# Graph attention with layer norm: both heads' quarters side by side in the moves, loads and stores of two tiles

## The chip, the cores and the metric

The kernel runs on one core of one Trainium2 chip. The metric is device microseconds of one launch; the kernel before took 1819.06 us, the median of three runs.

## What is computed

The reference, cut to what matters. There are 8 graphs of 1024 nodes with 384 features, 6 heads of 64 features, and a dense mask of 1024 x 1024 per graph.

```python
q = heads(x @ Wq + bq); k = heads(x @ Wk + bk); v = heads(x @ Wv + bv)
scores = einsum('bhqd,bhkd->bhqk', q, k) / sqrt(64)
probs = softmax(scores + where(adj, 0, -9e15), axis=-1)
ctx = einsum('bhqk,bhkd->bhqd', probs, v)
out = layernorm(x + merge(ctx) @ Wf + bf)
```

All data is float32. Projections and scores are built from three products of rounded high parts and low rests.

## The kernel before

The work of a batch (one graph) is cut into 24 slots. A slot is 128 queries of one pair of heads: slot `s` has group of queries `s // 6` (256 queries), pair `s % 6 // 2` and query tile `s % 2`. Two slots that share a pair and a group of queries make one mix (`GROUPS`, 12 in a batch). The batches are three bodies of program text: the first batch, a loop over six, and the last batch.

In a slot PE makes the scores of both heads (L494, `score_ps`, 128 x 1024 per head). DVE adds the mask and takes the row's minimum (`mask_scores`, L680), ACT takes the exponential and the row sum (`exponential`, L602), and DVE transposes every square of 32 x 32 in place (`turn_squares`, L688). All three work in `prob`, a ring of three slots with two rows of 1024 keys per partition, one for each head.

A whole transposition also needs the squares to change places between partitions. That is done by DMA: `move_square(queue, s, a, c)` (L290 to L295) takes 32 partitions and a quarter of the keys (256) of both heads from `prob`, and puts them into 32 other partitions of `prob_t`. There are 16 such moves in a slot, one for each pair of source quarter `a` and target quarter `c`. SP issues the twelve with `a != c` (`move`, L331), ACT the four with `a == c` (L612). Each move raises `landed[ring]` by 16. PE then mixes: for 8 tiles of keys and 2 heads it multiplies `prob_t` with `v_all` (`mix`, L499 to L512), each time with a moving operand of 8 runs of 32 columns.

The order of everything else is written out by hand. `STEADY` says which projections, mixes (`m`), spreads of the inverse row sums (`i`) and output projections (`p`) stand in which slot on PE; ACT, DVE and GpSimd follow the same table. SP's queue has, behind the moves of a slot, what four tables and a rule give it, one tile (128 rows) at a time: `load_adjacency` at slots 0 and 1 of every six, `X_LOADS`, `STORES`, `RES_LOADS`. Every one of them waits on a semaphore first, and everything queued behind on SP waits with it:

- `move` waits for DVE's squares (`squared`), and in even slots for the mix of two groups before (`mixed`), since `prob_t` has two halves;
- `store` (L358) waits for GpSimd's scaling of the tile (`normalised`, L286), which `NORMALISE` puts at slots 3, 10, 13 and 18;
- `load_residual` (L351) waits for the store from the same place, `load_x` (L341) for the transpositions on PE that read `x_in`, `load_adjacency` (L325) for GpSimd's mask from the same tile.

DVE's mask of a slot waits for the moves of the slot three before (`landed`), since it writes the same place of the ring.

Of the kernel before, what the change touches and what calls it, by code (L numbers as in the profile page):

```python
# [104 lines left out]
def graph_attention(nc, x, adj, wq, bq, wk, bk, wv, bv, wf, bf, out):  # L105
# [15 lines left out]
    with ExitStack() as ctx:  # L121
# [19 lines left out]
        prob = sb("prob", [P, 2 * RING, S], F32)  # L141
        prob_t = sb("prob_t", [P, 2, 2, 2, 4, GQ], F32)
# [25 lines left out]
        bv_wide = prob[:, 2 * RING - 1, 0:FT * P].rearrange("p (t n) -> p t n", t=FT)  # L168
# [13 lines left out]
        x_loaded = [sem(f"x_loaded{i}") for i in range(4)]  # L182
        res_loaded = [sem(f"res_loaded{g}") for g in range(4)]
        adj_loaded = [sem(f"adj_loaded{i}") for i in range(2)]
# [97 lines left out]

        def scale_rows(engine, group):
# [18 lines left out]
        def _(sp):  # L302
# [4 lines left out]
            for i in range(4):  # L307
                sp.dma_start(x_in[:, i, :], x_tiles[0, :, i, :]).then_inc(x_loaded[i], 16)
            for g in (2, 3):
                sp.dma_start(res[:, 2 * g:2 * g + 2, :], x_tiles[0, :, 2 * g:2 * g + 2, :]).then_inc(res_loaded[g], 32)  # L310
# [4 lines left out]
            for qt in range(2):  # L315
                sp.dma_start(adj_in[:, qt, :], adj_rows[qt * P:(qt + 1) * P, :]).then_inc(adj_loaded[qt], 16)
# [3 lines left out]
            for g in range(2):  # L320
                sp.dma_start(res[:, 2 * g:2 * g + 2, :], x_tiles[0, :, 2 * g:2 * g + 2, :]).then_inc(res_loaded[g], 32)
# [19 lines left out]
            def load_x(b, half, i):  # L341
                last_x = ("x", FT - 1, 1 - half, 1)
                if half == 0 and b.mode == "first":
                    sp.wait_ge(job_done, 3)
                else:
                    sp.wait_ge(job_done, done_through(b, last_x, 1 - half))
                    sp.sem_inc(sp_waited, 1)
                row = S + (4 * half + i) * P
                sp.dma_start(x_in[:, i, :], x_rows[bass.ds(at(b, S, row), P), :]).then_inc(x_loaded[i], 16)  # L349

            def load_residual(b, group, tile, ahead):  # L351
                sp.wait_ge(stored[group], at(b, 32, 32 * ahead))
                sp.sem_inc(sp_waited, 1)
                n = 2 * group + tile
                sp.dma_start(res[:, n, :], x_rows[bass.ds(at(b, S, ahead * S + n * P), P), :]  # L355
                             ).then_inc(res_loaded[group], 16)

            def store(b, group, tile):  # L358
                sp.wait_ge(normalised, at(b, TT, 2 * group + tile + 5))
                sp.sem_inc(sp_waited, 1)  # L360
                n = 2 * group + tile
                sp.dma_start(out_rows[bass.ds(at(b, S, n * P), P), :], res[:, n % TT, :]).then_inc(stored[group % 4], 16)  # L362

            def body(b):
                for s in range(SLOTS):
                    move(b, s)
                    if s % 6 < 2 and (s // 6 < 3 or b.mode != "last"):
                        load_adjacency(b, s // 6, s % 6)
                    if s in X_LOADS and b.mode != "last":
                        load_x(b, *X_LOADS[s])  # L370
                    if s in STORES and (STORES[s][0] >= 0 or b.mode != "first"):
                        store(b, *STORES[s])
                    if s in RES_LOADS:
                        group, tile = RES_LOADS[s]
                        if group >= 2 and b.mode != "first":
                            load_residual(b, group, tile, 0)
                        if group < 2 and b.mode != "last":
                            load_residual(b, group, tile, 1)
# [6 lines left out]
            for group in (2, 3):  # L385
                for tile in range(2):
                    store(last, group, tile)
            for g in range(4):
                sp.wait_ge(stored[g], 32 * BATCH)
# [3 lines left out]
        def _(pe):  # L393
# [66 lines left out]
            def run(b, job):  # L460
                bank_free(b, job)
                kind, n, piece, ahead = job
                if kind == "x":
                    if n == 0:
                        for i in range(4):
                            pe.wait_ge(x_loaded[i], at(b, 32, 16 * piece + 32) if piece == 0 else at(b, 32, 48))
# [32 lines left out]
            def mix(b, group):  # L499
# [25 lines left out]
            for n, job in enumerate(START_JOBS):  # L525
                if n == 0:
                    for i in range(4):
                        pe.wait_ge(x_loaded[i], 16)
                if n == 3:
                    for g in (2, 3):  # L530
                        pe.wait_ge(res_loaded[g], 32)
# [22 lines left out]
        def _(act):  # L554
# [42 lines left out]
            def exponential(b, t):  # L597
# [4 lines left out]
                nc.scalar.activation(prob[:, ring, :], prob[:, ring, :], ACT.Exp, scale=-1.0,  # L602
# [49 lines left out]
        def _(dve):  # L652
# [18 lines left out]
            def mask_scores(b, t):  # L671
# [8 lines left out]
                nc.vector.tensor_tensor_reduce(prob[:, ring, :], score_ps[:, head, :], mask[:, s % 2, :],  # L680
# [3 lines left out]
            def turn_squares(b, t):  # L684
                ring = 2 * (t // 2 % RING) + t % 2
# [86 lines left out]
        def _(pool):  # L772
# [8 lines left out]
            def next_mask(b, group, qt):  # L781
                pool.wait_ge(adj_loaded[qt], at(b, 64, 16 * (group + 1)))
# [4 lines left out]
            def residual(b, g):  # L787
                pool.wait_ge(res_loaded[g], at(b, 32, 32))
# [77 lines left out]
            nc.gpsimd.memset(ones[:], 1.0).then_inc(ones_done, 1)  # L866
            for qt in range(2):
                pool.wait_ge(adj_loaded[qt], 16)
# [28 lines left out]
```

## Time and profile before

| | us |
|---|---|
| median of three runs | 1819.06 |
| the three runs | 1817.99, 1819.06, 1821.70 |
| the profiled execution | 1816.15 |
| its span, first to last instruction | 1814.0 |

The profile is of one execution. Its span leaves out 2.15 us around the program. "Busy" counts the instructions of an engine, not its semaphore, register and DMA-issuing work; an engine's queue is written with a q (SPq, ACTq), and the chain and the timelines do show the time that it takes to issue a DMA. Line numbers are those of the kernel before.

### The profile page before, as it was taken

Reading aid. Unit: us, or ns where it says so; the run is one execution under the profiler, and the core shown is the slowest. Engines: PE = TensorE matmul, PEld = TensorE weight load, DVE = VectorE, ACT = ScalarE, POOL = GpSimd, SP = SyncE. Lnnn points to the kernel's source line nnn. Section 1 sums busy time; section 2 is a strip of 40 time slices with the busy share of each in tenths; the row PEclk is TensorE's granted clock in tenths of the full one; section 3 lists DMA queues with packets and bytes.
Section 4 is the critical chain, followed back from the end, with each engine's and each line's share of the span. In section 5 each row is a group of like instructions: output and inputs, shape, how many; then the busy total and the mean of one; then the engine's idle time right before and its main releaser. Section 6 shows DMA issues by size and latency. Waiting matters only on the chain.

```text
span 1814.0 us, 29642 instructions
## 1 busy us (share of the span) xinstructions
PE 1345.2 (74%) x8406; PEld 951.3 (52%) x8406; DVE 1059.9 (58%) x1617; ACT 722.3 (40%) x1404; POOL 655.0 (36%) x958
## 2 busy tenths in 40 slices
PE   7767796767967689676886677866888667887773
PEld 5545574545745457444574455644556445565542
DVE  5565665655656546565555655556556565566752
ACT  5443542434434434344443434434344344443330
POOL 2233541434314433154331543325433154342332
PEclk9897998878988889888898878978789788898977
DMA  5555555555555555555555555555555555555552
GB/s 154 138 136 146 144 136 141 135 151 143 128 140 140 148 139 126 142 138 149 143 128 143 139 143 141 128 140 142 146 139 132 141 146 143 144 130 149 144 137 78
DMA packets 285113, 251.62 MB, mean 139 GB/s; under 512 B 54400, under 2 KB 284928, under 8 KB 284928
## 3 DMA queue, kind: packets, MB, share of 16 engines
q1 hardware_dynamic: 223488, 199.07, 43.1%
q10 hardware_dynamic: 61440, 50.38, 11.4%
q8 instruction: 80, 1.31, 0.3%
q14 instruction: 105, 0.86, 0.2%
HBM read 35.33 MB, written 12.58 MB: 26 GB/s over the span
## 4 chain that ended last, share of the span: by engine, by line
SPq 76%; issue 10%; PE 5%; DVE 2%; ACTq 2%; ACT 2%; DMA 1%; POOL 1%; POOLq 0%; DVEq 0%
SPq L293 70%; PE context_ps L510 2%; ACTq L293 2%; DVE prob L688 2%; SPq L362 1%; SPq L329 1%; SPq L355 1%; PE score_ps L494 1%; DMA prob_t<-prob 1%; ACT prob L602 1%; SPq L349 1%; PE job_ps L399 0%; DMA x_in<-in_x_dram 0%; PE job_ps L401 0%; PE job_ps L400 0%
## 5 line engine op out<-in xcount | busy, mean ns | idle before, releaser
L510 PE MATMUL context_ps<-prob_t,v_all 128*64 128x256 f32 x3072 | 490.8, 489 | 306.5 <-DMA prob_t<-prob 306.4
L602 ACT ACTIVATE prob<-prob,row_min 128x1024 f32<-128x1024 f32 x384 | 439.6, 1146 | 530.5 <-DVE row_min L680 462.8
L680 DVE CUSTOM_DVE_ANT_0 prob<-score_ps,mask 128x1024 f32<-128x1024 f32 x384 | 454.2, 1220 | 214.0 <-PE score_ps L494 162.8
L510 PEld LDWEIGHTS context_ps<-prob_t,v_all 128*64 128x64 f32 x3072 | 301.3, 180 | 496.2 <-issue 386.7
L688 DVE STREAM_TRANSPOSE prob<-prob 128x1024 f32<-128x1024 f32 x384 | 457.9, 1231 | 151.4 <-ACT prob L602 151.4
L809 POOL TENSOR_TENSOR diag<-ident,inv_sum 128x512 f32<-128x512 f32 x96 | 99.9, 1040 | 488.4 <-DVE inv_sum L693 487.0
L610 ACT ACTIVATE context_hi<-context 128x256 fp32r<-128x256 f32 x96 | 40.1, 418 | 510.2 <-DVE context L698 385.5
L698 DVE TENSOR_TENSOR context<-context_ps,context 128x256 f32<-128x256 f32 x96 | 40.1, 418 | 317.6 <-PE context_ps L510 317.6
L803 POOL TENSOR_TENSOR q_lo<-raw,q_hi 128x256 fp32r<-128x256 f32 x95 | 69.3, 730 | 360.0 <-ACT raw L594 360.0
L399 PE MATMUL job_ps<-xt_hi,weight_hi 128*128 128x256 f32 (+1 forms) x423 | 149.4, 353 | 24.6 <-ACT raw L592 24.0
L494 PE MATMUL score_ps<-k_hi,q_hi 64*128 64x512 f32 x768 | 145.3, 457 | 20.6 <-DVE row_min L680 16.5
L401 PE MATMUL job_ps<-xt_hi,weight_lo 128*128 128x256 f32 (+1 forms) x423 | 137.1, 324 | 0.0
L400 PE MATMUL job_ps<-xt_lo,weight_hi 128*128 128x256 f32 (+1 forms) x423 | 137.0, 324 | 0.0
L494 PE MATMUL score_ps<-k_lo,q_hi 64*128 64x512 f32 x768 | 123.5, 399 | 0.0
L494 PE MATMUL score_ps<-k_hi,q_lo 64*128 64x512 f32 x768 | 122.5, 396 | 0.0
L399 PEld LDWEIGHTS job_ps<-xt_hi,weight_hi 128*128 128x128 f32 x423 | 80.9, 191 | 71.6 <-issue 36.7
L286 POOL TENSOR_SCALAR res<-res,mean_var,inv_dev 128x384 f32<-128x384 f32 x64 | 105.0, 1647 | 6.9 <-POOL inv_dev L834 6.9
L430 PE MATMUL job_ps<-diag,ones 128*64 128x256 f32 x384 | 67.8, 434 | 53.4 <-POOL diag L809 53.4
L494 PEld LDWEIGHTS score_ps<-k_hi,q_hi 64*128 64x128 f32 x768 | 59.5, 192 | 83.4 <-issue 60.8
L815 POOL TENSOR_TENSOR context_lo<-context,context_hi 128x256 fp32r<-128x256 f32 x96 | 70.5, 735 | 84.8 <-ACT context_hi L610 84.8
L803 POOL TENSOR_TENSOR k_lo<-raw,k_hi 128x512 fp32r<-128x512 f32 x46 | 58.3, 1288 | 116.1 <-ACT raw L594 116.1
L401 PEld LDWEIGHTS job_ps<-xt_hi,weight_lo 128*128 128x128 f32 x423 | 81.3, 192 | 6.7
(72 smaller groups left out, 1709.2 us busy)
## 6 DMA issues: line engine op xcount, KB each, us to landing
prob_t<-prob SPq DMA_DIRECT2D x2304, 64.0 KB, 2.0
prob_t<-prob ACTq DMA_DIRECT2D x768, 64.0 KB, 2.1
out_dram<-res SPq DMA_DIRECT2D x64, 192.0 KB, 2.1
x_in<-in_x_dram SPq DMA_DIRECT2D x60, 192.0 KB, 2.6
res<-in_x_dram SPq DMA_DIRECT2D x56, 192.0 KB
adj_in<-in_adj_dram SPq DMA_DIRECT2D x64, 128.0 KB, 2.1
res<-in_x_dram SPq DMA_DIRECT2D x4, 384.0 KB
prob_t<-in_L_gnn_Wk_dram SPq DMA_DIRECT2D x1, 576.0 KB, 3.9
```

Source lines behind the costliest of these rows:

```text
L286: engine.tensor_scalar(res[:, n, :], res[:, n, :], mean_var[:, group % 2, tile, 0:1], inv_dev[:, group % 2, tile:tile + 1], ALU.subtract, ...
L293: queue.dma_start(prob_t[32 * c:32 * c + 32, group % 2, :, qt, a, :], prob[32 * a:32 * a + 32, 2 * ring:2 * ring + 2, GQ * c:GQ * c + GQ]) ...
L399: pe.matmul(dst, left_hi, right_hi, start=(t == 0), stop=False)
L400: pe.matmul(dst, left_hi, right_lo, start=False, stop=False)
L401: last = pe.matmul(dst, left_lo, right_hi, start=False, stop=(t == FT - 1))
L494: last[head] = pe.matmul(score_ps[:, head, keys], q_part[rows, pair, q], k_part[rows, pair, keys], start=(n == 0), stop=(n == 2))
L510: last = pe.matmul(context_ps[64 * head:64 * head + 64, 0:GQ], v_all[:, kt, col:col + HS], keys, start=(kt == 0), stop=(kt == TT - 1))
L602: nc.scalar.activation(prob[:, ring, :], prob[:, ring, :], ACT.Exp, scale=-1.0, bias=row_min[:, ring:ring + 1], accum_out=row_sum[:, s // ...
L680: nc.vector.tensor_tensor_reduce(prob[:, ring, :], score_ps[:, head, :], mask[:, s % 2, :], 1.0, HUGE, ALU.add, ALU.min, row_min[:, ring:r ...
L688: nc.vector.transpose(prob[:, ring, :], prob[:, ring, :]).then_inc(squared, 1)
L803: nc.gpsimd.tensor_tensor(lo, copy[:, 0:width], hi, ALU.subtract).then_inc(lo_done, 1)
L809: nc.gpsimd.tensor_tensor(diag[:], ident[:].unsqueeze(1).to_broadcast([P, 4, P]), inv_sum[:, group % 2, :].unsqueeze(2).to_broadcast([P, 4 ...
```

## The change

`prob` is laid out anew: ring, quarter of keys, head, 256 keys. What a move takes from one partition, a quarter of both heads, is then one run of 512 numbers (2 KB) instead of two of 256. `prob_t` is laid out alike, so that it is one run there too. The number of moves, their bytes, their queues and their order stay. DVE's mask and transposition and ACT's exponential address a head as four pieces of 256 instead of one of 1024, and PE's moving operand steps over 512 numbers between its runs of 32 instead of 256.

Besides, loads of x, of residuals and of adjacency, and the stores, take two tiles (256 rows) in one issue. The tables say at which slots; most pairs go where their second tile went. The semaphores count accordingly.

```diff
-STORES = {5: (-2, 0), 6: (-2, 1), 12: (-1, 0), 13: (-1, 1), 15: (0, 0), 16: (0, 1), 19: (1, 0), 20: (1, 1)}
-RES_LOADS = {8: (2, 0), 9: (2, 1), 14: (3, 0), 15: (3, 1), 18: (0, 0), 19: (0, 1), 22: (1, 0), 23: (1, 1)}
-X_LOADS = {1: (0, 0), 2: (0, 1), 3: (0, 2), 4: (0, 3), 11: (1, 0), 12: (1, 1), 13: (1, 2), 14: (1, 3)}
+STORES = {5: -2, 12: -1, 16: 0, 20: 1}
+RES_LOADS = {8: 2, 15: 3, 19: 0, 23: 1}
+X_LOADS = {2: (0, 0), 4: (0, 1), 11: (1, 0), 14: (1, 1)}
...
-        prob = sb("prob", [P, 2 * RING, S], F32)
-        prob_t = sb("prob_t", [P, 2, 2, 2, 4, GQ], F32)
+        prob = sb("prob", [P, RING, 4, 2, GQ], F32)
+        prob_t = sb("prob_t", [P, 2, 2, 4, 2, GQ], F32)
...
+        def probabilities(t):
+            return prob[:, t // 2 % RING, :, t % 2, :]
...
-            queue.dma_start(prob_t[32 * c:32 * c + 32, group % 2, :, qt, a, :],
-                            prob[32 * a:32 * a + 32, 2 * ring:2 * ring + 2, GQ * c:GQ * c + GQ]
+            queue.dma_start(prob_t[32 * c:32 * c + 32, group % 2, qt, a].rearrange("p h n -> p (h n)"),
+                            prob[32 * a:32 * a + 32, ring, c].rearrange("p h n -> p (h n)")
                             ).then_inc(landed[ring], 16)
...
-            def load_adjacency(b, group, qt):
-                sp.wait_ge(mask_done, at(b, TT, 2 * group + qt + 1))
+            def load_adjacency(b, group):
+                sp.wait_ge(mask_done, at(b, TT, 2 * group + 2))
                 sp.sem_inc(sp_waited, 1)
-                row = (group + 1) * GQ + qt * P
-                sp.dma_start(adj_in[:, qt, :], adj_rows[bass.ds(at(b, S, row), P), :]).then_inc(adj_loaded[qt], 16)
+                sp.dma_start(adj_in[:], adj_rows[bass.ds(at(b, S, (group + 1) * GQ), GQ), :].rearrange(
+                    "(q p) k -> p q k", p=P)).then_inc(adj_loaded, 16)
...
-            def store(b, group, tile):
-                sp.wait_ge(normalised, at(b, TT, 2 * group + tile + 5))
+            def store(b, group):
+                sp.wait_ge(normalised, at(b, TT, 2 * group + 6))
                 sp.sem_inc(sp_waited, 1)
-                n = 2 * group + tile
-                sp.dma_start(out_rows[bass.ds(at(b, S, n * P), P), :], res[:, n % TT, :]).then_inc(stored[group % 4], 16)
+                n = 2 * group
+                sp.dma_start(out_rows[bass.ds(at(b, S, n * P), GQ), :].rearrange("(t p) h -> p t h", p=P),
+                             res[:, n % TT:n % TT + 2, :]).then_inc(stored[group % 4], 16)
...
-                    if s % 6 < 2 and (s // 6 < 3 or b.mode != "last"):
-                        load_adjacency(b, s // 6, s % 6)
+                    if s % 6 == 1 and (s // 6 < 3 or b.mode != "last"):
+                        load_adjacency(b, s // 6)
...
-                        keys = prob_t[:, group % 2, head, :, :, 32 * kt:32 * kt + 32].rearrange(
+                        keys = prob_t[:, group % 2, :, :, head, 32 * kt:32 * kt + 32].rearrange(
...
-                nc.scalar.activation(prob[:, ring, :], prob[:, ring, :], ACT.Exp, scale=-1.0,
+                nc.scalar.activation(probabilities(t), probabilities(t), ACT.Exp, scale=-1.0,
...
-                nc.vector.tensor_tensor_reduce(prob[:, ring, :], score_ps[:, head, :], mask[:, s % 2, :],
+                nc.vector.tensor_tensor_reduce(probabilities(t), in_quarters(score_ps[:, head, :]),
+                                               in_quarters(mask[:, s % 2, :]),
...
-                nc.vector.transpose(prob[:, ring, :], prob[:, ring, :]).then_inc(squared, 1)
+                nc.vector.transpose(probabilities(t), probabilities(t)).then_inc(squared, 1)
```

`load_x` and `load_residual` are changed as `store` is. How SP's queue reads is shown at one place, slots 12 and 13 of the loop body, where loads of adjacency and of x and a store stand behind the moves. "ISA" and "REGISTER_ALU" rows are work on the registers that carry addresses and semaphore values. Before:

```order
L293 DMA prob_t<-prob 32x2x256 x12
L326 REGISTER_ALU
L329 ISA
L329 DMA adj_in<-in_adj_dram 128x1024
L349 ISA
L349 DMA x_in<-in_x_dram 128x384
L362 ISA
L362 DMA out_dram<-res 128x384
L332 REGISTER_ALU
L293 DMA prob_t<-prob 32x2x256 x12
```

And now (L301 is the move, L371 the store, L336 the adjacency):

```order
L301 DMA prob_t<-prob 32x512 x12
L371 ISA
L371 DMA out_dram<-res 128x2x384
L340 REGISTER_ALU
L301 DMA prob_t<-prob 32x512 x12
L334 REGISTER_ALU
L336 ISA
L336 DMA adj_in<-in_adj_dram 128x2x1024
L340 REGISTER_ALU
L343 REGISTER_ALU
L301 DMA prob_t<-prob 32x512 x12
```

After slot 12 stood three issues of one tile and stands one of two; the adjacency has gone to slot 13, where three more stood before. On DVE no instruction changes its place; the two that work in `prob` change their shape. Before:

```order
L680 ISA prob,row_min<-score_ps,mask 128x1024
L680 ISA row_min 128x1
L680 ISA prob,row_min<-score_ps,mask 128x1024
L680 ISA row_min 128x1
L688 STREAM_TRANSPOSE prob<-prob 128x1024 x2
```

And now, in the first slot of the first batch like the rows above:

```order
L689 ISA prob,row_min<-score_ps,mask 128x4x256
L689 ISA row_min 128x1
L689 ISA prob,row_min<-score_ps,mask 128x4x256
L689 ISA row_min 128x1
L697 STREAM_TRANSPOSE prob<-prob 128x4x256 x2
```

The same five instructions, a head in four pieces.

## Rows read from the trace of the kernel before

**Rows 1.** The page's head and part 1: engine, busy us (share) xinstructions.

```profile
span 1814.0 us, 29642 instructions
...
PE 1345.2 (74%) x8406; PEld 951.3 (52%) x8406; DVE 1059.9 (58%) x1617; ACT 722.3 (40%) x1404; POOL 655.0 (36%) x958
```

**Rows 2.** The page, part 4: the chain that ended last, by engine, by line.

```profile
SPq 76%; issue 10%; PE 5%; DVE 2%; ACTq 2%; ACT 2%; DMA 1%; POOL 1%; POOLq 0%; DVEq 0%
SPq L293 70%; PE context_ps L510 2%; ACTq L293 2%; DVE prob L688 2%; SPq L362 1%; SPq L329 1%; SPq L355 1%; PE score_ps L494 1%; DMA prob_t<-prob 1%; ACT prob L602 1%; SPq L349 1%; PE job_ps L399 0%; DMA x_in<-in_x_dram 0%; PE job_ps L401 0%; PE job_ps L400 0%
```

**Rows 3.** Waits of SP's queue: who waited for whom: us in total, times, longest.

```profile
SPq L360 <- POOL res L286: 21.0, 4, 13.7
SPq L334 <- DVE prob L688: 19.1, 1, 19.1
SPq L293 <- DVE prob L688: 3.4, 9, 0.7
```

**Rows 4.** By source line: engine, issue xcount: ns min/median/max, first and last start.

```profile
L293 SPq DMA_DIRECT2D prob_t<-prob x2304: 585/597/1980, 32.3 to 1788.7; - x192
L293 ACTq DMA_DIRECT2D prob_t<-prob x768: 592/619/2363, 33.5 to 1780.7; - x192
...
L349 SPq DMA_DIRECT2D x_in<-in_x_dram x56: 337/346/586, 49.4 to 1502.5; - x56
...
L355 SPq DMA_DIRECT2D res<-in_x_dram x56: 333/344/1095, 198.7 to 1722.0; - x56
...
L362 SPq DMA_DIRECT2D out_dram<-res x64: 332/365/1112, 171.9 to 1811.7; - x64
```

**Rows 5.** SP's timeline, in three windows: start us, us, queue, line, xcount merged.

```profile
953.67 7.97 SPq L293 DMA_DIRECT2D prob_t<-prob  x12
...
1016.00 8.34 SPq L293 DMA_DIRECT2D prob_t<-prob  x12
...
1025.29 8.66 SPq L293 DMA_DIRECT2D prob_t<-prob  x12
1034.28 0.33 SPq L329 DMA_DIRECT2D adj_in<-in_adj_dram  x1
1034.89 0.34 SPq L349 DMA_DIRECT2D x_in<-in_x_dram  x1
1035.50 0.36 SPq L362 DMA_DIRECT2D out_dram<-res  x1
1035.98 7.66 SPq L293 DMA_DIRECT2D prob_t<-prob  x12
```

**Rows 6.** By source line: the prologue's single tiles (L308) and double tiles (L321).

```profile
L308 SPq DMA_DIRECT2D x_in<-in_x_dram x4: 432/432/475, 1.3 to 2.7; - x4
...
L321 SPq DMA_DIRECT2D res<-in_x_dram x2: 466/468/469, 12.0 to 12.5; - x2
```

**Rows 7.** DMA queues: packets, MB, share; whole span, then 1027 to 1029 us.

```profile
q1 hardware_dynamic: 223488, 199.07, 43.1%
q10 hardware_dynamic: 61440, 50.38, 11.4%
...
q8 instruction: 1, 0.02, 3.7%
```

**Rows 8.** The page, part 5, three groups: busy us, mean ns | idle before.

```profile
L510 PE MATMUL context_ps<-prob_t,v_all 128*64 128x256 f32 x3072 | 490.8, 489 | 306.5 <-DMA prob_t<-prob 306.4
...
L680 DVE CUSTOM_DVE_ANT_0 prob<-score_ps,mask 128x1024 f32<-128x1024 f32 x384 | 454.2, 1220 | 214.0 <-PE score_ps L494 162.8
...
L688 DVE STREAM_TRANSPOSE prob<-prob 128x1024 f32<-128x1024 f32 x384 | 457.9, 1231 | 151.4 <-ACT prob L602 151.4
```

**Rows 9.** Timelines of PE (first row) and DVE, in three windows.

```profile
945.63 3.62 PE L510 MATMUL context_ps<-prob_t,v_all 128*64 128x256 f32 x32
...
1012.62 2.39 DVE L688 STREAM_TRANSPOSE prob<-prob 128x1024 f32<-128x1024 f32 x2 [0.28 <-ACT prob L602]
...
1026.74 2.39 DVE L688 STREAM_TRANSPOSE prob<-prob 128x1024 f32<-128x1024 f32 x2 [0.28 <-ACT prob L602]
```

More of the change, by code:

```diff
@@ L181, in graph_attention @@
         ones_done = sem("ones_done")
-        x_loaded = [sem(f"x_loaded{i}") for i in range(4)]
+        x_loaded = [sem(f"x_loaded{i}") for i in range(2)]
         res_loaded = [sem(f"res_loaded{g}") for g in range(4)]
-        adj_loaded = [sem(f"adj_loaded{i}") for i in range(2)]
+        adj_loaded = sem("adj_loaded")
         mask_done = sem("mask_done")
@@ L281, in job_parts, with in_quarters @@
             return GQ, q_hi[:, pair, :], q_lo[:, pair, :]
+        def probabilities(t):
+            return prob[:, t // 2 % RING, :, t % 2, :]
+        def in_quarters(keys):
+            return keys.rearrange("p (c n) -> p c n", c=4)
         def scale_rows(engine, group):
@@ L306, in _ @@
             load_weight(1, wk)
-            for i in range(4):
-                sp.dma_start(x_in[:, i, :], x_tiles[0, :, i, :]).then_inc(x_loaded[i], 16)
+            for i in range(2):
+                sp.dma_start(x_in[:, 2 * i:2 * i + 2, :], x_tiles[0, :, 2 * i:2 * i + 2, :]).then_inc(x_loaded[i], 16)
             for g in (2, 3):
-                sp.dma_start(res[:, 2 * g:2 * g + 2, :], x_tiles[0, :, 2 * g:2 * g + 2, :]).then_inc(res_loaded[g], 32)
+                sp.dma_start(res[:, 2 * g:2 * g + 2, :], x_tiles[0, :, 2 * g:2 * g + 2, :]).then_inc(res_loaded[g], 16)
             load_weight(0, wq)
@@ L347, in load_x, with load_residual @@
                     sp.sem_inc(sp_waited, 1)
[L348 to L352, printed above, removed]
-                sp.sem_inc(sp_waited, 1)
-                n = 2 * group + tile
-                sp.dma_start(res[:, n, :], x_rows[bass.ds(at(b, S, ahead * S + n * P), P), :]
-                             ).then_inc(res_loaded[group], 16)
-            def store(b, group, tile):
-                sp.wait_ge(normalised, at(b, TT, 2 * group + tile + 5))
+                row = S + (4 * half + 2 * i) * P
+                sp.dma_start(x_in[:, 2 * i:2 * i + 2, :], x_rows[bass.ds(at(b, S, row), GQ), :].rearrange(
+                    "(t p) h -> p t h", p=P)).then_inc(x_loaded[i], 16)
+            def load_residual(b, group, ahead):
+                sp.wait_ge(stored[group], at(b, 16, 16 * ahead))
+                sp.sem_inc(sp_waited, 1)
+                n = 2 * group
+                sp.dma_start(res[:, n:n + 2, :], x_rows[bass.ds(at(b, S, ahead * S + n * P), GQ), :].rearrange(
+                    "(t p) h -> p t h", p=P)).then_inc(res_loaded[group], 16)
+            def store(b, group):
+                sp.wait_ge(normalised, at(b, TT, 2 * group + 6))
                 sp.sem_inc(sp_waited, 1)
-                n = 2 * group + tile
-                sp.dma_start(out_rows[bass.ds(at(b, S, n * P), P), :], res[:, n % TT, :]).then_inc(stored[group % 4], 16)
+                n = 2 * group
+                sp.dma_start(out_rows[bass.ds(at(b, S, n * P), GQ), :].rearrange("(t p) h -> p t h", p=P),
+                             res[:, n % TT:n % TT + 2, :]).then_inc(stored[group % 4], 16)
             def body(b):
@@ L366, in body @@
                     move(b, s)
-                    if s % 6 < 2 and (s // 6 < 3 or b.mode != "last"):
-                        load_adjacency(b, s // 6, s % 6)
+                    if s % 6 == 1 and (s // 6 < 3 or b.mode != "last"):
+                        load_adjacency(b, s // 6)
                     if s in X_LOADS and b.mode != "last":
                         load_x(b, *X_LOADS[s])
-                    if s in STORES and (STORES[s][0] >= 0 or b.mode != "first"):
-                        store(b, *STORES[s])
+                    if s in STORES and (STORES[s] >= 0 or b.mode != "first"):
+                        store(b, STORES[s])
                     if s in RES_LOADS:
-                        group, tile = RES_LOADS[s]
+                        group = RES_LOADS[s]
                         if group >= 2 and b.mode != "first":
-                            load_residual(b, group, tile, 0)
+                            load_residual(b, group, 0)
                         if group < 2 and b.mode != "last":
-                            load_residual(b, group, tile, 1)
+                            load_residual(b, group, 1)
             body(Batch("first", 0, 0))
@@ L385, in _ @@
             for group in (2, 3):
-                for tile in range(2):
-                    store(last, group, tile)
+                store(last, group)
             for g in range(4):
-                sp.wait_ge(stored[g], 32 * BATCH)
+                sp.wait_ge(stored[g], 16 * BATCH)
         @block.tensor
@@ L464, in run @@
                     if n == 0:
-                        for i in range(4):
-                            pe.wait_ge(x_loaded[i], at(b, 32, 16 * piece + 32) if piece == 0 else at(b, 32, 48))
+                        for i in range(2):
+                            pe.wait_ge(x_loaded[i], at(b, 32, 16 * piece + 32))
                     transpose_x(b.mode, job)
@@ L526, in _ @@
                 if n == 0:
-                    for i in range(4):
+                    for i in range(2):
                         pe.wait_ge(x_loaded[i], 16)
@@ L530, in _ @@
                     for g in (2, 3):
-                        pe.wait_ge(res_loaded[g], 32)
+                        pe.wait_ge(res_loaded[g], 16)
                 if n >= 4:
@@ L781, in next_mask @@
             def next_mask(b, group, qt):
-                pool.wait_ge(adj_loaded[qt], at(b, 64, 16 * (group + 1)))
+                pool.wait_ge(adj_loaded, at(b, 64, 16 * (group + 2)))
                 pool.wait_ge(masked, at(b, UNITS, 12 * group + 2 * qt))
```

11 lines of the change are left out of this document (5 added, 6 removed).

## The prediction

> **What bounds the kernel now.** I read the busy shares, then the chain that ended last, then the waits of SP's queue, then the issues on SP one by one. No engine is near full: PE is busy for 74% of the span [rows 1]. The chain, however, lies for 76% on SP's queue, and for 70% on the one line that issues the moves of probability squares [rows 2]. SP's own waits are nearly nil: 19.1 us once, for the first squares, 21.0 us in the tail for the last stores, 3.4 us in 9 waits for DVE elsewhere [rows 3]. From its first move at 32.3 us to its last at 1788.7 us [rows 4] SP issues without a pause: 2304 moves, and between them 117 x 2 = 234 loads and stores (56 + 56 + 60, four of the 64 stores coming after the last move, and 62 adjacency loads like the one at 1034.28) [rows 4, 5]. Twelve undisturbed moves take 7.66 us, 0.64 us from one to the next [rows 5], 0.597 us in the instruction and the rest between [rows 4].
>
> The engines wait for SP: PE stood 306.5 us ahead of the mixing matmuls until moves had landed [rows 8]. How late SP is can be read in one slot: DVE has turned its squares at 1012.62 + 2.39 = 1015.01 us and SP takes them up at 1016.00, 1.0 us later. Two slots on, the squares are ready at 1029.13 and SP comes at 1035.98, 6.9 us later [rows 5, 9]. Even slots also wait for a mix: it ends at 945.63 + 3.62 = 949.25 and SP comes at 953.67, 4.4 us late [rows 5, 9]. So **the time is what SP has to issue**, and everything else has between 1 and 7 us of cover per slot. The DMA engines are not the limit: the two queues fill 43.1% and 11.4% of them [rows 7].
>
> **Loads and stores, two tiles at a time.** 117 issues vanish between the first move and the last. Three in a row start at 1034.28, 1034.89 and 1035.50: 0.61 us each, register work and semaphore event included [rows 5]. Six of eight batches run in the loop at that price: 16 x 6 = 96 issues x 0.61 = 58.6 us. The other 21 lie in the unrolled batches, where an issue is dearer (the largest static ones in rows 4 and 6 are 0.43 to 0.59) but has no register work; I take 0.57: 12.0 us. Together 70.5 us, all of it on SP, thus all of it on the path.
>
> The 117 that stay carry two tiles. In the prologue, single tiles cost 0.432 us each and double ones 0.468 [rows 6]: 0.036 x 117 = 4.2 us back. Net **66.3 us**.
>
> **Waits that move.** SP now stores a pair at the slot where it stored the first tile (slots 5 and 12), and waits there for the second one. Queued behind that wait would be the next slot's twelve moves, and DVE and PE behind these. But GpSimd scales a pair's two tiles one behind the other, and the whole waiting of SP for them is 21.0 us in 4 times, which is the tail [rows 3]; elsewhere no store waited, so I cost this at nothing. The cover is that normalising is placed slots ahead, at slots 3 and 10. The adjacency pair is issued at the second slot of a group instead of one tile at each; GpSimd needs the first tile in the fifth. Loads of x and of residuals keep the slot of their last tile, and the earlier slot is used only where what they overwrite is long free. In the tail the last pair leaves in one store after the second tile; at most half a microsecond, left out.
>
> **Where the gain is lost.** SP can't run ahead of DVE. Where its lateness is only 1.0 us, a saving larger than that turns into a wait. That slot (eleven in a batch) has one issue fewer in the three before it, 0.6 us: covered, just. In the first batch, where SP started by waiting, three issues (1.8 us) before slot 4 save nothing. I put 3 us for both. Net: 66.3 - 3 = 63 us.
>
> **The moves.** Their number and bytes stay, 2304 on SP and 768 on ACT. A move now has 32 runs of 2 KB where it had 64 of 1 KB. The trace has no such move, and the sum hangs on its price: 10 ns a move is 23 us. From above: it stays at 0.597, ACT's being 0.619 [rows 4]. From below: the cheapest issues in a row, 0.432 [rows 6], or 0.346 for a lone one [rows 4]. Which is nearest? Issues of 128 runs are cheaper than the moves' of 64, and two tiles cost nearly what one costs: the price doesn't go by runs or by bytes, but by something that these loads have and moves between two places in SBUF have not. The change leaves moves what they are in that. I take 0.597, unchanged, so 0 us.
>
> 70 of SP's 2304 moves take over 0.9 us. Rows 5 and 7 show one: the twelve moves from 1025.29 take 8.66 us where others take 7.66, and from 1027 to 1029 us the instruction queue loads a piece (q8). I leave that 1 us each as it is.
>
> On the DMA engines, ACT's 61440 packets take 0.114 x 16 x 1814 us, 54 ns each on average [rows 7]. Fewer, longer packets lighten engines that are 55% full; landing may come a tenth of a microsecond earlier, in front of waits that SP's pace sets. 0 us. [...]
>
> **The engines.** DVE's mask and transposition and ACT's exponential now go over four pieces of 256 rather than one of 1024, and PE's moving operand steps 2 KB instead of 1 KB between runs of 32. Rows 8 give mask, transposition and mixing matmul today: 1220, 1231 and 489 ns [rows 8]. A few per cent more (below 0.1 us each, five in a slot) vanish in the cover of mostly 4 to 7 us; they would show only at slot eleven, 6 to 8 times, 2 us in all. Below zero there is nothing to gain.
>
> **Sum.** Profiled span 1814.0 - 63 = 1751 us; its run 1816.15 - 63 = 1753; the median of the runs shown, 1819.06, lies 2.9 above that run, so 1819 - 63 = 1756. I say **1755 us**.
>
> **Rivals.**
> 1. *The move gets cheaper to issue* with one run per partition. For it: 64 runs become 32 and a dimension goes. Against: the double tiles in rows 6, which have that dimension and 256 runs, cost only 36 ns more. If a dimension is worth those 36 ns to a move too: 2304 x 0.036 = 83 us more, 1672. If the price fell to 0.432 it would be 380 us, and SP would no longer be the bound; then what is left is at least the span less PE's wait for moves, 1814 - 306 = 1508, and with the rings of three slots nearer 1580.
> 2. *The stalls at code loading shrink*, as fewer packets stand in the rings behind the long one. For: the stall is there only with such a piece. Against: the prologue queues packets for 384 KB and more at 0.47 us an issue without one [rows 6]. 70 stalls at 1 us; half of that gone: 1720.
> 3. *A double tile costs as two*: 117 x 0.345 = 40 us come back, 70.5 - 40 - 3 = 27, so 1792. Rows 6 speak against it.
> 4. *Nothing comes of it*, 1819: the saved issue time is taken up at once by waits for DVE and PE. It needs the lateness in rows 9 to be small nearly everywhere; it is in one slot. [...]
> 5. *Slower*: a move's issue takes longer, since the queue must hand each DMA engine 2 KB runs. From 63 / 2304 = 27 ns on, a price of 0.624, it eats the gain; at 0.66 us the kernel takes 1755 + 145 = 1900. For it: ACT's moves already cost 0.619 and the 1.0 us stalls show that a queue can be held up by long packets. Against: prologue loads with longer runs are cheaper, not dearer.
>
> **Chances.** Forecast 0.64; rival 1 0.13 (0.05 of it far below 1672); rival 2 0.08; rival 3 0.04; rival 4 0.05; rival 5 0.06. Faster by over 0.2% (what a measurement of this kernel can tell from no change): 0.64 + 0.13 + 0.08 + 0.04 = 0.89; within: 0.05; slower: 0.06. The range from 1670 to 1792 takes in the forecast with its price of a move off by up to 15 ns either way (35 us), rivals 2 and 3, and rival 1 down to 1672; its deep form and rivals 4 and 5 stay outside, 0.05 + 0.05 + 0.06 = 0.16.
>
> **What would show it.** SP's moves: 2304 with a median of 0.597. 117 fewer loads and stores, medians near 0.38 in the loop. SP's waits small still, some for DVE at slot eleven. A loop body 9.3 us shorter. Chain again for three quarters on SP. It would be wrong if the median of a move differs by more than 15 ns, if SP's waits grow to tens of microseconds, or if the mask, exponential or transposition grow by over a microsecond a slot.

## The result

The changed kernel takes **1729.66 us** (median of four runs, 1726.69 to 1730.98) against 1818.53 for the kernel before in the same comparison: a ratio of 0.951, 95% interval 0.949 to 0.953. The forecast was 1755, in a range of 1670 to 1792. The direction and the mechanism held; 89 us were gained where the sum had 63.

The page of the changed kernel, with the rows that answer to [rows 1, 2, 7, 8]: span, busy shares, the two DMA queues (packets, MB, share), the chain by engine and by line, and three groups (busy us, mean ns | idle before).

```profile
span 1728.6 us, 29185 instructions
...
PE 1326.2 (77%) x8406; PEld 948.2 (55%) x8406; DVE 1060.2 (61%) x1617; ACT 721.8 (42%) x1404; POOL 655.7 (38%) x958
...
q1 hardware_dynamic: 147824, 199.06, 44.1%
q10 hardware_dynamic: 36864, 50.38, 11.9%
...
SPq 79%; issue 9%; PE 4%; ACT 2%; DVE 2%; DMA 2%; ACTq 1%; POOL 1%; POOLq 0%; DVEq 0%
SPq L301 76%; PE context_ps L519 2%; DMA prob_t<-prob 1%; ACT prob L611 1%; DVE prob L697 1%; ACTq L301 1%; SPq L371 1%; PE score_ps L503 1%; SPq L357 1%; SPq L336 1%; SPq L364 1%; PE job_ps L408 0%; DMA x_in<-in_x_dram 0%; POOL res L294 0%; DVE weight_lo L758 0%
...
L519 PE MATMUL context_ps<-prob_t,v_all 128*64 128x256 f32 x3072 | 468.4, 472 | 239.8 <-DMA prob_t<-prob 239.8
...
L689 DVE CUSTOM_DVE_ANT_0 prob<-score_ps,mask 128x1024 f32<-128x1024 f32 x384 | 454.3, 1220 | 206.1 <-PE score_ps L503 168.4
L697 DVE STREAM_TRANSPOSE prob<-prob 128x1024 f32<-128x1024 f32 x384 | 457.9, 1231 | 148.9 <-ACT prob L611 148.9
```

DVE's mask and transposition cost what they did, to the nanosecond (1220 and 1231): going over four pieces instead of one is free here. PE's mixing matmul takes 472 ns instead of 489, at a mean granted clock of TensorE of 0.881 instead of 0.861. The DMA packets of SP's queue fell from 223488 to 147824, a third, and the time they fill on the DMA engines by little (43.1% of 1814 us, 44.1% of 1729). What changed on the engines is the waiting: PE stood 239.8 us ahead of the mixing matmuls for moves, 306.5 before. The chain still lies for 79% on SP's queue.

SP's own waits, which answer to [rows 3] (who waited for whom: us in total, times, longest):

```profile
SPq L369 <- POOL res L294: 22.2, 2, 15.6
SPq L342 <- DVE prob L697: 19.8, 1, 19.8
SPq L301 <- PE context_ps L519: 4.7, 4, 3.5
SPq L301 <- DVE prob L697: 2.8, 4, 1.9
```

Still almost nothing but start and tail. SP begins its first move at 32.2 us and its last at 1702.4; before it was 32.3 and 1788.7. So 86.2 us less of uninterrupted issuing, which is the gain. By source line, in the columns of [rows 4]:

```profile
L301 SPq DMA_DIRECT2D prob_t<-prob x2304: 507/591/2066, 32.2 to 1702.4; - x192
...
L301 ACTq DMA_DIRECT2D prob_t<-prob x768: 513/614/2306, 33.4 to 1695.1; - x192
...
L357 SPq DMA_DIRECT2D x_in<-in_x_dram x28: 378/379/692, 56.8 to 1426.4; - x28
...
L364 SPq DMA_DIRECT2D res<-in_x_dram x28: 380/386/1476, 202.5 to 1637.4; - x28
...
L371 SPq DMA_DIRECT2D out_dram<-res x32: 378/411/1922, 177.0 to 1725.6; - x32
```

Half the loads and stores, each about 0.04 us dearer. But the moves have changed too: the shortest was 0.585 us and is 0.507. A piece of SP's timeline shows which ones are short (the first two rows are single moves, the first and the fifth of one slot; then a load, the twelve moves of a slot, and a store):

```profile
1003.07 0.52 SPq L301 DMA_DIRECT2D prob_t<-prob  x1
...
1005.54 0.59 SPq L301 DMA_DIRECT2D prob_t<-prob  x1
...
1011.68 0.39 SPq L364 DMA_DIRECT2D res<-in_x_dram  x1
1012.31 7.71 SPq L301 DMA_DIRECT2D prob_t<-prob  x12
1020.29 0.41 SPq L371 DMA_DIRECT2D out_dram<-res  x1
```

The first move of a slot takes 0.52 us, those behind it 0.59. Over all 192 slots the median of the first is 0.518 (0.605 before), that of the fifth 0.591 (0.597 before). From the start of one move to the start of the next in a slot the median is 0.633 us, 0.639 before; the expectations below have 0.634 and 0.640 for these.

### The profile page after: what moved, and what is told of

It reads as the page before. It is cut to its first block, busy times and chain, and to the rows that moved or that the text cites. A ratio compares the mean times of both kernels' runs of the same rounds, so it can differ in the third digit from the quotient of the medians.

```text
span 1728.6 us, 29185 instructions
## 1 busy us (share of the span) xinstructions
PE 1326.2 (77%) x8406; PEld 948.2 (55%) x8406; DVE 1060.2 (61%) x1617; ACT 721.8 (42%) x1404; POOL 655.7 (38%) x958
## 3 DMA queue, kind: packets, MB, share of 16 engines
q1 hardware_dynamic: 147824, 199.06, 44.1%
## 4 chain that ended last, share of the span: by engine, by line
SPq 79%; issue 9%; PE 4%; ACT 2%; DVE 2%; DMA 2%; ACTq 1%; POOL 1%; POOLq 0%; DVEq 0%
SPq L301 76%; PE context_ps L519 2%; DMA prob_t<-prob 1%; ACT prob L611 1%; DVE prob L697 1%; ACTq L301 1%; SPq L371 1%; PE score_ps L503 1%; SPq L357 1%; SPq L336 1%; SPq L364 1%; PE job_ps L408 0%; DMA x_in<-in_x_dram 0%; POOL res L294 0%; DVE weight_lo L758 0%
## 5 line engine op out<-in xcount | busy, mean ns | idle before, releaser
L519 PE MATMUL context_ps<-prob_t,v_all 128*64 128x256 f32 x3072 | 468.4, 472 | 239.8 <-DMA prob_t<-prob 239.8
L689 DVE CUSTOM_DVE_ANT_0 prob<-score_ps,mask 128x1024 f32<-128x1024 f32 x384 | 454.3, 1220 | 206.1 <-PE score_ps L503 168.4
L697 DVE STREAM_TRANSPOSE prob<-prob 128x1024 f32<-128x1024 f32 x384 | 457.9, 1231 | 148.9 <-ACT prob L611 148.9
L519 PEld LDWEIGHTS context_ps<-prob_t,v_all 128*64 128x64 f32 x3072 | 294.6, 173 | 413.8 <-issue 298.3
L824 POOL TENSOR_TENSOR context_lo<-context,context_hi 128x256 fp32r<-128x256 f32 x96 | 70.5, 735 | 95.2 <-ACT context_hi L619 94.7
```

The lines of the kernel that those rows point to most:

```text
L519: last = pe.matmul(context_ps[64 * head:64 * head + 64, 0:GQ], v_all[:, kt, col:col + HS], keys, start=(kt == 0), stop=(kt == TT - 1))
L689: nc.vector.tensor_tensor_reduce(probabilities(t), in_quarters(score_ps[:, head, :]), in_quarters(mask[:, s % 2, :]), 1.0, HUGE, ALU.add, ...
L697: nc.vector.transpose(probabilities(t), probabilities(t)).then_inc(squared, 1)
```

## The experiments

Runs of one comparison share a chip. On the chips of all the following ones the kernel before took about 1810 us, and not 1818.53, and the changed kernel was not run there. So a change is given against the kernel before of the same comparison, or as a ratio. Where a run is set against the changed kernel, two figures are given: the plain difference to 1729.66, and the difference of the two ratios times 1810. They lie some 8 us apart, and nothing finer can be read from them.

**The two halves apart.** The first keeps the tables and the single tiles of before and changes only where things lie:

```diff
-        prob = sb("prob", [P, 2 * RING, S], F32)
-        prob_t = sb("prob_t", [P, 2, 2, 2, 4, GQ], F32)
+        prob = sb("prob", [P, RING, 4, 2, GQ], F32)
+        prob_t = sb("prob_t", [P, 2, 2, 4, 2, GQ], F32)
...
-            queue.dma_start(prob_t[32 * c:32 * c + 32, group % 2, :, qt, a, :],
-                            prob[32 * a:32 * a + 32, 2 * ring:2 * ring + 2, GQ * c:GQ * c + GQ]
+            queue.dma_start(prob_t[32 * c:32 * c + 32, group % 2, qt, a].rearrange("p h n -> p (h n)"),
+                            prob[32 * a:32 * a + 32, ring, c].rearrange("p h n -> p (h n)")
```

> The new layout of prob and prob_t alone, loads and stores one tile at a time as before. Theory A (the layout gives what the forecast left out; after's trace has the first move of a slot's twelve at a median of 0.518 us instead of 0.605 and the other eleven at 0.591 instead of 0.597): 192 x (0.087 + 11 x 0.006) = 29 us at most, so 1790 to 1800. Rival B (the 20 us come from elsewhere, for instance less contention of the moves with the loads because there are half as many of these): within 5 us of before, 1815 to 1820, with the first move at 0.605.

Measured: 1780.42 us against 1810.39, ratio 0.983 (0.979 to 0.987). The expected 1790 to 1800 counts from 1819, so it is 30 us of gain against the 29 at most of theory A. By source line:

```profile
L300 SPq DMA_DIRECT2D prob_t<-prob x2304: 507/591/2092, 30.0 to 1752.1; - x192
...
L356 SPq DMA_DIRECT2D x_in<-in_x_dram x56: 336/347/698, 46.8 to 1469.5; - x56
```

The second is the changed kernel with these lines put back, that is, with pairs of tiles and the old layout:

> Loads and stores two tiles at a time alone, with the layout of before. The forecast's sum (117 issues of 0.61 or 0.57 us gone, 0.036 us added to each that stays, 3 us lost to new waits) gives 1819 - 63 = 1756. Theory A: 1750 to 1758, and together with the layout alone it makes after's 89 us. Rival B: below 1740, as the pairs also make the moves cheaper.

Measured: 1752.32 us, ratio 0.968 (0.964 to 0.972).

```profile
L301 SPq DMA_DIRECT2D prob_t<-prob x2304: 585/597/2167, 30.5 to 1722.7; - x192
...
L357 SPq DMA_DIRECT2D x_in<-in_x_dram x28: 386/388/752, 56.2 to 1444.9; - x28
```

The product of the two ratios is 0.951, that of the whole change. The pairs alone are worth 58 us of 1810, the forecast's 63 of 1819 lying inside their interval; the layout alone is worth 30 us (23 to 39 by its interval), which the forecast had at nothing. The moves are short (0.507) where the layout is new and long (0.585) where it is old, whatever the loads do: theory A stands in both, rival B falls. The layout takes away half of a move's runs and one dimension of its pattern in one; no run parts these two.

**What sets the pace of a row of moves.** If the sequencer is through with a move in 0.51 us, as its shortest are (507 ns), why do the eleven behind the first take 0.59? An increment of a semaphore that nobody waits for was put behind each of SP's moves, once in the changed kernel and once in the kernel before:

```diff
                         if not (a == c):
                             move_square(sp, s, a, c)
+                            sp.sem_inc(sp_waited, 1)
```

> After, with one increment of a semaphore that nobody waits for on SP behind each of its 2304 moves (about 0.02 us in itself, some 0.065 with its gap). Theory C (in a row of moves the pace of 0.634 us is set outside the sequencer, which itself needs only the 0.51 us that a first move takes): the distance from move to move stays at 0.634, the moves themselves are shorter by about 0.06, and the time stays within 5 us of after. Rival D (the sequencer itself needs 0.591 us for every move but the first): the distance grows to 0.70 us, and the time by 2304 x 0.065 = 150 us less what waits absorb, 1850 or more.

Measured: 1734.88 us (one run), where the changed kernel takes 1729.66. By source line, and SP's timeline:

```profile
L301 SPq DMA_DIRECT2D prob_t<-prob x2304: 507/533/2297, 30.5 to 1705.6; - x192
...
1012.22 7.68 SPq L301 DMA_DIRECT2D prob_t<-prob  x12
```

Within a row the moves shrink by what the increment takes: 0.533 instead of 0.591, and the distance from one to the next stays at a median of 0.633. The twelve moves of a slot with their increments take 7.68 us here, and 7.71 without them in the changed kernel's timeline above. The increment itself is 0.017 us and adds 0.040 of gaps, 0.057 in all by the medians. Only at the edges of a slot is it paid: behind the first move the distance grows from 0.564 to 0.628, which is 12 us over 192 slots. The time is 5 us above 1729.66, or 14 by the ratios (0.958 and 0.951); one run can't part these. The 2304 x 0.065 = 150 us of rival D are out either way.

> The kernel before, with one increment of a semaphore that nobody waits for on SP behind each of its 2304 moves. In before a first move takes 0.605 us and the distance in a row is 0.640, which is what the sequencer alone would give (0.597 and a gap of 0.04). Theory C (two limits, the sequencer's own work at 0.64 in before and 0.55 in after, and a pace of 0.634 set outside it): here there is no room, the distance grows by about 0.065 to 0.70, and the time by 2304 x 0.06 = 140 us, to 1940 or more. Rival J (the layout has nothing to do with the room; the row's pace hides it in before too): distance 0.64, time within 10 us of before.

Measured: 1908.44 us (one run), 97 more than before.

```profile
L293 SPq DMA_DIRECT2D prob_t<-prob x2304: 585/586/2154, 30.2 to 1880.4; - x192
...
1029.61 7.46 SPq L293 DMA_DIRECT2D prob_t<-prob  x11
```

Here the moves shrink only from 0.597 to their shortest, 0.586, and the distance grows from 0.639 to 0.686, which times 2304 is 108 us. Rival J falls. I had expected 0.70 and 1940 us or more, taking 0.065 for the increment; it is 0.057, and 0.011 of that comes back from the shorter moves.

The two runs fit two limits: what the sequencer itself needs, and a slower pace that is kept by something other than its own work. My estimate of the need is the shortest instruction and the usual gap of 0.043: 0.586 + 0.043 = 0.629 us in the old layout, 0.507 + 0.043 = 0.550 in the new. A row of moves goes slower than that in both, at 0.639 and 0.633. Theory C, which took the whole 0.640 of before for the sequencer's own, was off in this: there was room for 0.010 us even there. The change took 0.079 off the need so estimated, and a row got only 0.006 of it, except in the first move of each slot, which comes after a pause. Whether the 0.010 of before and the 0.083 of now come from the same limit is not shown.

**Whether the pace goes by bytes.** Each move carries only head 0's quarter, 32 runs of 1 KB; PE mixes head 0's probabilities for both heads, so head 1's are left out.

```diff
-            queue.dma_start(prob_t[32 * c:32 * c + 32, group % 2, qt, a].rearrange("p h n -> p (h n)"),
-                            prob[32 * a:32 * a + 32, ring, c].rearrange("p h n -> p (h n)")
+            queue.dma_start(prob_t[32 * c:32 * c + 32, group % 2, qt, a, 0],
+                            prob[32 * a:32 * a + 32, ring, c, 0]
...
-                        keys = prob_t[:, group % 2, :, :, head, 32 * kt:32 * kt + 32].rearrange(
+                        keys = prob_t[:, group % 2, :, :, 0, 32 * kt:32 * kt + 32].rearrange(
```

> After, but each move carries the quarter of head 0 alone, 32 runs of 1 KB, and PE mixes head 0's probabilities for both heads; head 1's probabilities are left out of the output. Half the bytes, the same 32 runs. Theory E (an issue is priced per instruction, whatever it carries): a move at 0.59 in a row and 0.51 in front, time within 10 us of after. Rival F (the pace in a row goes by bytes): distance of 0.634 falls towards 0.51 + 0.04 = 0.55, 2304 x 0.08 = 180 us less, if no other wait takes over.

Measured: 1713.09 us (one run). By source line, and SP's DMA queue:

```profile
L301 SPq DMA_DIRECT2D prob_t<-prob x2304: 507/591/2114, 31.5 to 1683.5; - x192
...
q1 hardware_dynamic: 147824, 123.56, 25.7%
```

Half the bytes, a DMA share of 25.7% instead of 44.1%, and the very same 507 and 591 ns; the median distance in a row is 0.633 again. Rival F falls. The run is 17 us below 1729.66, more than the 10 that I had allowed, and 8 by the ratios (0.946 and 0.951). What SP's moves take beyond 0.6 us each sums to 67 us here against 84 in the changed kernel. The same sum is 65 in the layout alone and 81 in the pairs alone, so that it wanders by this much between executions; whether fewer bytes have a part in it can't be told from one.

Two more candidates are answered by traces at hand. The pace doesn't go by the number of runs in proportion: moves of 64 runs went at a median of 0.639 us in the kernel before and in the pairs alone, moves of 32 at 0.633 in the changed kernel and in the layout alone. And ACT's issuing next to it makes no such difference: from the fourth move of a slot on, the median distance to the next in the changed kernel is 0.634 us in the 640 places where ACT issues a move meanwhile, and 0.633 in the 896 where it doesn't; in the kernel before it is 0.640 (654 places) and 0.639 (882).

```diff
     nc = _bacc.Bacc("TRN2", target_bir_lowering=False, num_devices=1)
+    nc.dge_precook = False
```

> [...] Theory H (this mark is what makes loads cheaper than moves, 0.38 against 0.51 for one after a pause): the loads and stores rise to 0.51 or more, the moves stay, time 117 x 0.13 = 15 us more or up to 117 x 0.2 = 23. Rival I (they are cheaper because one side is HBM): they stay at 0.38.

Measured: 1769.85 us (one run), 40 above 1729.66, and 49 by the ratios (0.978 and 0.951).

```profile
L301 SPq DMA_DIRECT2D prob_t<-prob x2304: 507/591/2409, 32.6 to 1741.0; - x192
...
L357 SPq DMA_DIRECT2D x_in<-in_x_dram x28: 672/687/734, 57.9 to 1462.1; - x28
...
L364 SPq DMA_DIRECT2D res<-in_x_dram x28: 659/687/710, 204.1 to 1675.8; - x28
...
L329 SPq DMA_DIRECT2D res<-in_x_dram x2: 610/619/628, 11.9 to 12.5; - x2
```

A row of moves is as it was (591 ns a move, 0.633 us from one to the next; only the first of a slot goes from 0.518 to 0.546), the double loads go from 0.379 and 0.386 to 0.687 us, those of adjacency from 0.390 to 0.702, the stores from 0.411 to 0.711, and in the prologue it is 0.619 instead of 0.468 [rows 6]. Rival I falls. Theory H holds, with a price over twice what I had put: 117 x 0.30 = 35 us. In the profiled executions SP's loads and stores sum to 83.9 us instead of 52.2, and its moves to 5 us more. The same transfer in the same shape is 0.31 us dearer with the setting off (0.379 to 0.687 for x), and an issue of two tiles then takes longer than a move of one run, 0.687 against 0.591. Whether a move can be issued as cheaply as these loads was not tried.

**A faster version: moves given to ACT.** If issuing on SP is the time, ACT can take more of it. Three runs of the changed kernel, with one, two and three more of a slot's moves on ACT:

```diff
-                        if not (a == c):
-                            move_square(sp, s, a, c)
+                        if not (a == c or (a, c) == (0, 1)):
+                            move_square(sp, s, a, c)
...
-                        if a == c:
-                            move_square(act, s, a, c)
+                        if (a == c or (a, c) == (0, 1)):
+                            move_square(act, s, a, c)
```

The second adds (2, 3), the third (1, 0) as well.

> After, with one more of a slot's sixteen moves issued by ACT: 11 on SP, 5 on ACT. If SP's issuing is the time (theory A), each move taken off SP gives 192 x 0.634 = 122 us, less what SP then waits for DVE (it is 4.5 us late in the median slot of after, but 0.2 to 2.9 us at slot eleven): 1610 to 1640. Rival G (another engine or ring is already as near a bound): above 1700.

> After, with 10 moves of a slot on SP and 6 on ACT. SP alone would give 1730 - 243 = 1487; PE's span without its wait for moves in after is 1729 - 240 = 1489, ACT needs 722 + 6 x 0.64 x 192 = 1459 us of work and issuing. With three queues that near to each other the waits add up: 1530 to 1590. SP's waits for DVE and PE should be over 50 us in sum.

> After, with 9 moves of a slot on SP and 7 on ACT. ACT: 722 + 7 x 0.64 x 192 = 1582 us, SP below 1370. If ACT's issuing then is the bound, 1600 to 1680, slower than 10 and 6.

| moves of a slot on SP, ACT | us | ratio to before (95%) |
|---|---|---|
| 12, 4 (the changed kernel) | 1729.66 | 0.951 (0.949 to 0.953) |
| 11, 5 | 1652.87 | 0.912 (0.910 to 0.915) |
| 10, 6 | 1756.99 | 0.970 (0.967 to 0.974) |
| 9, 7 | 1864.31 | 1.029 (1.026 to 1.032) |

One move fewer on SP gave 77 us by the plain difference and 70 by the ratios, of the 122 that its issuing takes; I had expected 90 to 120, so this missed. The chain and SP's waits with 11 and 5:

```profile
SPq 42%; issue 18%; PE 12%; ACTq 9%; DVE 9%; ACT 5%; POOL 3%; DMA 2%; DVEq 0%; POOLq 0%
...
SPq L301 <- DVE prob L697: 22.1, 15, 3.7
SPq L342 <- DVE prob L697: 22.0, 8, 19.6
SPq L301 <- PE context_ps L519: 20.0, 7, 5.9
```

Outside the tail SP waits 64 us in sum, 19.6 of it at the start and the rest mostly at slots 4 and 11 of a batch: there the cover of a few microseconds that the forecast counted is used up. With 10 and 6 my estimate was off by about 200 us, and with 9 and 7 by as much (1600 to 1680 expected, 1864 measured). The chain of 10 and 6, one of DVE's waits, and SP's:

```profile
ACTq 36%; issue 20%; DVE 19%; ACT 12%; PE 9%; POOL 3%; DVEq 1%; DMA 0%; SPq 0%; POOLq 0%
...
DVE prob L697 <- ACT prob L611: 514.5, 192, 7.0
...
SPq L342 <- DVE prob L697: 127.8, 88, 19.6
SPq L301 <- DVE prob L697: 106.2, 78, 5.5
SPq L301 <- PE context_ps L519: 71.1, 15, 9.2
```

SP is now the one that waits, 305 us, and the chain has gone to ACT's issuing. ACT stands in its order until DVE has turned a slot's squares, then issues six moves, which take a median of 4.0 us from the start of the first to the end of the last, while DVE masks the next slot, and DVE waits for ACT's exponentials, 514.5 us in all. I had added ACT's busy time and its issuing and left out that this circle of steps has to be gone through one after another in each slot.

That account was put to the test by letting ACT issue a slot's moves one slot later, behind the next exponentials:

```diff
-                    if s < SLOTS:
-                        move(b, s)
+                    if 0 < s < SLOTS:
+                        move(b, s - 1)
+                    if s == SLOTS - 1:
+                        move(b, s)
```

> 11 moves of a slot on SP and 5 on ACT, and ACT issues a slot's moves one slot later, behind the next slot's exponentials, so that it doesn't stand and wait for DVE's squares. Theory K (with 5 and more moves on ACT its order is the bound, as it waits for the squares, then issues while DVE's next mask is ready): ACT is freed, SP's waits shrink from 65 us, 1610 to 1650. Rival L (later landing of ACT's part makes mask and mix wait): above 1653.

> 10 on SP and 6 on ACT, with ACT's moves one slot later. Theory K: well below 1757, the time of 10 and 6 without the delay, and near or below late5: 1560 to 1650. Rival L, or issuing as such being what ACT has no time for: 1700 or more.

Measured: 1644.03 us with 11 and 5, ratio 0.908 (0.906 to 0.911), and 1656.15 us with 10 and 6, ratio 0.913 (0.910 to 0.916). The chain of the first:

```profile
span 1635.3 us, 29191 instructions
...
SPq 36%; PE 23%; issue 14%; DMA 8%; ACT 7%; ACTq 7%; DVE 4%; POOL 1%; DVEq 0%; POOLq 0%
```

and of the second, with DVE's wait for ACT:

```profile
span 1657.1 us, 29191 instructions
...
PE 34%; issue 16%; ACTq 15%; ACT 11%; SPq 9%; DMA 8%; DVE 4%; POOL 1%; DVEq 0%; POOLq 0%
...
DVE prob L699 <- ACT prob L611: 148.6, 192, 4.9
```

Without the wait for squares 10 and 6 lose 101 us, and DVE's wait for ACT's exponentials falls from 514.5 us to 148.6, what it was in the changed kernel (148.9). So it was ACT's order that had held them up; theory K stands there, 6 us outside its range of 1560 to 1650. With 11 and 5 the delay gains 7 to 9 us, at the edge of what the two intervals can tell apart, and SP's waits did not shrink as theory K had it: they sum to 63 us, 64 without the delay. The chain now goes through SP, PE's mixing and scores, landing DMAs and ACT in turn: there is no single queue left to relieve. With 11 and 5 and the delay the kernel has the lowest time of this study.

## Why the prediction was right, and where its size was off

**What bounds the kernel.** Right. SP's queue almost without pause from 32 us on, and the time follows it: 86.2 us less issuing, 89 us less time; a move a slot taken off it gives 70 to 77 us more; 0.30 us added to each of its 117 loads and stores costs 40 to 49.

**The 117 issues.** The forecast took 70.5 us off and put 4.2 back. Summed over SP's instructions between first and last move, the loads and stores fell from 95.8 to 52.2 us, register and semaphore work from 30.3 to 20.3, gaps from 177.2 to 165.0: together 65.8. A double tile is 0.033 to 0.046 us dearer than a single one (0.346 to 0.379 for x, 0.365 to 0.411 for stores), where 0.036 was taken. Rival 3, a double tile at the price of two, falls. A loop body is 12.0 us shorter (223.4 to 211.4 from first move to first move); the forecast's sign said 9.3, where its own terms, 16 x 0.61 less 16 x 0.036, give 9.2, and the moves add the rest.

**The waits.** Right: no store waited outside the tail. The gaps above 0.15 us grew by 7.3 us in all, 3.9 of it at the loop's branch (14.8 to 18.6 us over the six passes), where 3 was forecast for waits. Counted slot by slot, SP's lateness fell from a median of 6.0 to 4.5 us, and at slot eleven of the loop bodies from between 0.9 and 3.0 to between 0.2 and 2.9: covered, just.

**The engines.** Right, and nothing at all, where up to 2 us had been allowed.

**The moves: the term that was mis-sized.** It was put at 0 and measured 20.4 us in the two profiled executions (1453.7 us of moves, then 1433.3), or 30 us by the run with the layout alone. 192 firsts by 0.087 and 2112 others by 0.006 make 29 us; 5 us more in long stalls take some back in this execution. The step that failed is the one that carried the price from loads to moves. The range held because it allowed 15 ns either way on a move, not because this was foreseen: by the two profiled executions it was 9 ns a move on average, by the run with the layout alone 13.

**The other rivals.** The stalls at code loading (rival 2) did not shrink: 70 of SP's moves took over 0.9 us before, 75 do now. 69 of the 70 and all of the 75 coincide with a piece on the instruction queue (q8), of which there are 80 in both. So the stalls stay as they were with packets twice as long and half as many. Nothing came of rival 5; the median of a move fell. Rival 4 falls with the 89 us.

SP's DMA queue, with moves of 2 KB runs instead of 1 KB, filled the DMA engines for 762 us (44.1% of 1728.6) instead of 782 (43.1% of 1814.0). The gain of a longer run lay in the issuing. A single move's issue is short beside the transfer, 0.59 us against a median of 2.0 from issue to landing (the last figure of this row); the time of this kernel goes by the issuing even so, since a move a slot given to ACT changes nothing but who issues it and where in that queue, and gave 70 to 77 us.

```profile
prob_t<-prob SPq DMA_DIRECT2D x2304, 64.0 KB, 2.0
```

## What to carry to other kernels

Look at a DMA-issuing queue as at an engine: if its own waits are nearly nil, the chain lies on it and it has thousands of issues, its instructions times their price are the kernel's time, and halving the number of loads pays even where no byte is saved (58 us of 1810 here). Before a price is carried from one kind of DMA to another, see that both are issued in the same way: one setting moved the double loads from 0.379 to 0.687 us and left a row of moves at 0.591. The first of a row and those behind it are two different prices as well, 0.518 and 0.591 us here. And when work is moved to a second queue, ask what that queue has to wait for in its order, not only how busy it is: DVE's wait for ACT was 514.5 us with six moves on ACT, and 148.6 with their issue one slot later.

## What was not expected of the hardware

In these runs a row of moves between two places in SBUF, one run of 1 or 2 KB a partition, went at one per 0.633 us on SP, whether 32 or 64 KB were carried and whether or not the sequencer had 0.057 us of other work between them. With two runs a partition it went at 0.639. What keeps this pace is not settled. It isn't bytes (0.633 with half of them), nor ACT's moves beside it (0.634 with one, 0.633 without); for the loads it doesn't hold, as two in a row start less than 0.5 us apart in [rows 6] (four of them from 1.3 to 2.7 us). Inside a row of the changed kernel's moves, therefore, a semaphore increment was free; in the kernel before, with two runs a partition, 0.047 of its 0.057 us was paid.
